# Routed experts: weights loaded once per expert, results gathered back after the last block

## The chip, the cores and the metric

The kernel runs on one core of a Trainium2 chip. The metric is the time of one execution in device microseconds (us); the median of several runs is compared.

## The reference, cut to what matters

A decoder of 12 stages (4 layers of attention, cross attention and feed-forward) adds to a residual of 1024 rows by 256, all float32. Three feed-forward stages are mixtures of experts: layer 0 (here l0f: 16 experts, the 6 best per token), layer 2 (l2f: 8 experts, 2 best, and a shared expert in 4 parts for all tokens) and layer 3 (l3f: 64 experts, 4 best). For l3f:

```python
router_probs = jax.nn.softmax((x @ gate_weight.T).astype(jnp.float32), axis=-1)
top_v, top_i = jax.lax.top_k(router_probs, 4)
top_v = top_v / jnp.clip(top_v.sum(axis=-1, keepdims=True), 1e-12)
combine = jnp.zeros((T, E), dtype=top_v.dtype).at[jnp.arange(T)[:, None], top_i].add(top_v)
gate, up = jnp.split(x @ w1.T, 2, axis=-1)
out += (jax.nn.silu(gate) * up @ w2.T) * combine[:, expert][:, None]
```

## The kernel before, in words

Each stage is a block of code with one program per engine: TensorE (PE), ScalarE (ACT), VectorE (DVE), GpSimd (POOL) and SyncE (SP), which issues most DMAs. Semaphores order them. `experts` (L613) builds the three mixture stages.

**The router.** The normalised tokens h (8 tiles of 128 rows) are stored to the DRAM tensor h_rows by SP. DVE and PE find each token's best experts, count how many blocks of 128 rows each expert needs (blocks sorted by expert), the owner of each block, a slot for each of a token's K choices, and for each block the list of its tokens. The owners are spread over one partition by a matmul against a diagonal and copied to `owners`; SP reads them one by one into a register. The number of groups of four blocks depends on the data; each engine reads it with `group_count` (a value load, L802). Here l0f has 56 blocks (14 groups), l2f 20 (5), l3f 64 (16).

**The blocks.** Each engine walks over the groups with its own `step` four times per group; `by_steps` (L600) writes out the first group, puts the others in a loop (`Fori`, its branch at L606) and the pipeline's end after it. Of a block:
- POOL gathers its 128 rows of h_rows by an indirect DMA (L868), four buffers x;
- PE transposes them (L964, after the wait for x at L962 and for xT), ACT copies them to xT (L1016);
- PE multiplies with the expert's w_in (L973), ACT takes silu of one half (L1022), DVE multiplies it with the other (L1152);
- PE transposes that (L982), DVE copies it (L1146), PE multiplies with w_down (L992), DVE copies y (L1160) and ACT stores it to the stage's DRAM tensor y_rows (L1027).

PE works on four blocks at a time, each a stage further: the transpose of block b stands beside w_in of b-1, the second transpose of b-2 and w_down of b-3.

**The weights.** SP reads the owner of the next block (L821), waits until its place in the ring (16, 16 or 32 places) is free (L827) and until the transfer before on that semaphore has landed (L831), and issues w_in and w_down (L832): one pair per block, whichever expert it is. Before these it stores h and fills that part of y_rows which may stay without a block (L815 to L817: 4, 2 and 16 DMAs of 512 KB), so that every row gathered later is finite.

**The results.** After the last x gather POOL reads, for each choice c, the last block that holds a c-th choice, waits until it is stored (L884 to L887), and issues eight indirect gathers of y_rows (L892), one per tile of tokens, into up to 24 buffers (`BACKS`: 8 own ones, 8 in h and 8 in hT). Only the last choice waits for all blocks. DVE, after its last y, picks the weights of the choices and accumulates each gathered tile into the residual (L1176). The stage ends with the last accumulate.

## Time and profile before

| | |
|---|---|
| median of 3 runs | 1965.07 us (1960.84 to 1971.27) |
| the profiled execution | 1945.26 us |
| its span in the profile | 1943.4 us |
| granted TensorE clock, mean | 0.807 of full speed |
| PE busy | 1126.4 us (58%) |
| DVE busy | 1129.1 us (58%) |
| POOL busy | 591.0 us (30%) |
| DMA | 196.56 MB, mean 101 GB/s |

The profile was taken of a single execution, so its times stand against 1945.26, not against the median. Busy shares are averages over 12 stages with different limits. All times are microseconds from the span's start. A row of a timeline gives start, duration, engine, line, operation, output<-inputs, and in brackets how long the engine was idle before it and what ended the idle time ("issue": nothing that the profile shows). PE's and SP's sequencers (PEldq, SPq) have rows of their own. The expert stages lie at about 264 to 521 (l0f), 1245 to 1412 (l2f) and 1690 to 1932.5 us (l3f).

### The profile page before, as it was taken

The numbers are of one execution on the slowest core, as the hardware profiler recorded it, in microseconds if no ns is written. First come the engines' busy times: TensorE is split into PE (matmuls) and PEld (weight loads), VectorE is DVE, ScalarE is ACT, GpSimd is POOL, SyncE is SP. The second block draws the span as 40 slices with busy tenths as digits, with TensorE's granted clock in tenths as the row PEclk, the third lists the DMA queues.
The fourth block names the chain that finished last, engine by engine and source line by source line (L and its number), as shares of the span: only waits on it lengthen the run. The fifth ranks groups of instructions, "written<-read, shape, count | busy, mean of one in ns | idle before, by whom it ended". The sixth has DMA issues, their size and how long they took to land. (4 is left out here: it accounts for less than half of the span.)

```text
span 1943.4 us, 22726 instructions
## 1 busy us (share of the span) xinstructions
PE 1126.4 (58%) x5644; PEld 710.2 (37%) x5644; DVE 1129.1 (58%) x1878; ACT 473.7 (24%) x881; POOL 591.0 (30%) x616
## 2 busy tenths in 40 slices
PE   5316548994073962551696703698566278648750
PEld 2202125772042730111454502576433034437530
DVE  5759974442462637998875694411457358464324
ACT  2143302220021533320211101332122146403210
POOL 0026613445610103661100072034402022115454
PEclk9669967996586975996898856899878579969985
DMA  6024329983209002421000011244300620088762
GB/s 209 1 90 146 113 77 283 320 285 93 65 9 185 5 27 85 151 87 65 1 0 1 1 13 30 88 134 144 93 5 0 149 49 3 3 279 255 227 192 85
DMA packets 146199, 196.56 MB, mean 101 GB/s; under 512 B 35056, under 2 KB 109954, under 8 KB 145484
## 3 DMA queue, kind: packets, MB, share of 16 engines
q1 hardware_dynamic: 109996, 144.47, 25.3%
q0 software_dynamic: 12608, 31.26, 5.7%
q10 hardware_dynamic: 23520, 19.93, 3.3%
q8 instruction: 35, 0.57, 0.1%
q14 instruction: 40, 0.33, 0.1%
HBM read 153.55 MB, written 41.75 MB: 100 GB/s over the span
## 5 line engine op out<-in xcount | busy, mean ns | idle before, releaser
L163 PE MATMUL psum<-w_ident,h 128*128 128x128 f32 x144 | 32.5, 419 | 156.5 <-DVE h L144 156.5
L1530 DVE TENSOR_REDUCE l3x_neg<-psum 128x2 f32<-128x512 f32 x128 | 80.8, 683 | 59.6 <-PE psum L1402 59.6
L453 PE MATMUL psum<-l0s_conv_out,w_ident 128*128 128x512 f32 x128 | 65.0, 632 | 83.5 <-DVE l0s_conv_out L550 83.5
L453 PE MATMUL psum<-l1s_conv_out,w_ident 128*128 128x512 f32 x128 | 65.4, 636 | 80.0 <-DVE l1s_conv_out L550 80.0
L1505 ACT ACTIVATE l3x_work<-psum 128x512 f32<-128x512 f32 x128 | 72.5, 599 | 75.2 <-PE psum L1424 74.9
L175 ACT ACTIVATE hT<-psum 128x512 f32<-128x512 f32 x40 | 21.7, 595 | 281.2 <-PE psum L163 239.4
L152 POOL TENSOR_SCALAR rstd<-moments 128x8 f32<-128x8 f32 x12 | 2.9, 240 | 281.3 <-DVE moments L140 281.3
L163 PEld LDWEIGHTS psum<-w_ident,h 128*128 128x128 f32 x144 | 29.0, 222 | 160.2 <-DVE h L144 148.0
L419 POOL TENSOR_TENSOR l0s_xpad<-l0s_du,l0s_bc 128x1024 f32<-128x1024 f32 x32 | 75.3, 2354 | 32.5 <-DVE psum L546 32.3
L419 POOL TENSOR_TENSOR l1s_xpad<-l1s_du,l1s_bc 128x1024 f32<-128x1024 f32 x32 | 75.2, 2353 | 32.5 <-DVE psum L546 32.4
L973 PE MATMUL psum<-l0f_w_in,l0f_xT 128*128 (+1 forms) x224 | 78.5, 474 | 11.3 <-issue 11.1
L973 PE MATMUL psum<-l3f_w_in,l3f_xT 128*128 (+1 forms) x256 | 60.1, 360 | 41.1 <-issue 18.0
L868 POOL DMA_INDIRECT l3f_x<-l3f_h_rows,l3f_token_now x64 | 61.5, 961 | 62.7 <-PE psum L964 48.6
L546 DVE TENSOR_TENSOR_SCAN psum<-psum,l0s_xpad 128x1024 f32<-128x1024 f32 x32 | 73.2, 2286 | 5.3 <-POOL l0s_xpad L419 5.3
L546 DVE TENSOR_TENSOR_SCAN psum<-psum,l1s_xpad 128x1024 f32<-128x1024 f32 x32 | 73.2, 2286 | 5.2 <-POOL l1s_xpad L419 5.2
L1146 DVE COPY l0f_gatedT<-psum 88x256 f32<-88x256 f32 x56 | 23.6, 421 | 83.9 <-PE psum L982 49.1
L868 POOL DMA_INDIRECT l0f_x<-l0f_h_rows,l0f_token_now x56 | 53.9, 962 | 60.2 <-PE psum L964 43.4
L1146 DVE COPY l3f_gatedT<-psum 96x128 f32<-96x128 f32 x64 | 18.4, 288 | 91.9 <-PE psum L982 41.2
L453 PEld LDWEIGHTS psum<-l0s_conv_out,w_ident 128*128 128x128 f32 x128 | 22.2, 193 | 126.3 <-DVE l0s_conv_out L550 110.4
L453 PEld LDWEIGHTS psum<-l1s_conv_out,w_ident 128*128 128x128 f32 x128 | 22.4, 195 | 123.3 <-DVE l1s_conv_out L550 107.2
L1402 PE MATMUL psum<-l3x_k_packed,l3x_q_packed 48*128 48x256 bf16 x256 | 43.1, 306 | 34.9 <-DMA l3x_q_packed<-l3x_parts 31.0
L1530 DVE TENSOR_REDUCE l1a_neg<-psum 128x3 f32<-128x384 f32 x64 | 34.6, 556 | 47.1 <-PE psum L1410 46.8
(641 smaller groups left out, 3218.9 us busy)
## 6 DMA issues: line engine op xcount, KB each, us to landing
l0f_w_in<-in_l0f_w_in SPq DMA_DIRECT2D x56, 352.0 KB
l0s_bc<-l0s_scratch SPq DMA_DIRECT2D x16, 1024.0 KB, 5.1
l1s_bc<-l1s_scratch SPq DMA_DIRECT2D x16, 1024.0 KB, 5.2
l3f_w_in<-in_l3f_w_in SPq DMA_DIRECT2D x64, 192.0 KB
l0f_w_down<-in_l0f_w_down SPq DMA_DIRECT2D x56, 176.0 KB
l2f_w_in<-in_l2f_w_in SPq DMA_DIRECT2D x24, 352.0 KB
l3f_y_rows<-h SPq DMA_DIRECT2D x16, 512.0 KB, 6.8
l3f_y_rows<-l3f_y ACTq DMA_DIRECT2D x64, 128.0 KB
```

The lines of the kernel that those rows point to most:

```text
L152: m.pool_order.link(pool, nc.gpsimd.tensor_scalar(m.rstd[:, 0, :], m.moments[:, :, 1], EPS, None, ALU.add))
L163: ins = nc.tensor.transpose(m.psum[:, at:at + P], m.h[:, t, k * P:(k + 1) * P], m.ident[:])
L175: nc.scalar.activation(m.hT[:, k, cols], m.pair(k)[:, cols], ACT.Copy).then_inc(m.hT_ready, 1)
L419: nc.gpsimd.tensor_tensor(drive[c], du[:, c, :], bc[s][:, 0, :], ALU.mult).then_inc(drive_ready, 1)
L453: ins = nc.tensor.matmul(m.pair(2 + c)[:, cols], lhsT=m.ident[:], rhs=rhs[:, cols], start=start, stop=stop, skip_group_check=True)
L546: nc.vector.tensor_tensor_scan(state[c], decay[c], drive[c], 0.0, ALU.mult, ALU.add).then_inc(scanned, 1)
L868: nc.gpsimd.indirect_dma_start(x[s][:], None, h_rows, bass.IndirectOffsetOnAxis(ap=token_now[s // 2][:, s % 2:s % 2 + 1], axis=0)).then_in ...
L973: ins = nc.tensor.matmul(in_ps[d % 2], lhsT=xT[d % 2][:, k, :], rhs=w_in[:, bass.ds(place(base + d), 1), k, :].rearrange("p o x -> p (o x) ...
L1146: nc.vector.tensor_copy(gatedT[d % 2][:], gT_ps[d % 2]).then_inc(gT_ready, 1)
L1402: ins = nc.tensor.matmul(out[:, qt * S:(qt + 1) * S], lhsT=q[:, qt * P:(qt + 1) * P], rhs=k, start=True, stop=True)
L1505: nc.scalar.activation(self.prob[i % 8][:, 0:self.keys], self.bank(3 + i % 3)[:, 0:self.keys], ACT.Exp).then_inc(self.exp_done, 1)
L1530: ins = nc.vector.tensor_reduce(self.neg[k % 2][:, :, hl], bank[:, 0:self.keys].rearrange("p (q k) -> p q k", q=self.maxima), AX_X, ALU.ma ...
```

## The change

- SP loads the weights of every expert once per stage (16, 12 and 64 pairs), at the stage's start and without the owners; at most four experts are in flight, and the semaphore `there` counts the experts that have arrived.
- PE reads the expert of each block itself: two value loads per group of four blocks, each of a word that packs four experts (6 bits each), one for the w_in blocks and one for the w_down blocks, which lag by another two. They stand at the head of the group, ahead of the wait for x, and once more after the loop. Per block PE waits for `there`. The waits for in_loaded and down_loaded go.
- The words are made by one matmul with a constant (`packing`) instead of the diagonal.
- All back gathers wait until all y are stored. Buffers for them: 24, 16 and 16, those in h and hT first.
- y_rows becomes one DRAM tensor for all stages, and all of it (24 DMAs of 512 KB) is filled in stage 0 on SP, after the weight loads, out of ctxT.
- The store of h goes from SP's queue to ACT's, ahead of Exp.
- To make room in SBUF, routing buffers share memory: combine with probs; rest, goes, before, over and slots with hT; picked, x, y and xT with the routing tables; the memset of `before` moves behind the router's matmul. "carry" and "ctxT" leave the group "consts" for a group "spans" that is dropped after stage 10.

```diff
+            m.wait_weights(sp, "spans")
+            for rows in m.y_rows.rearrange("(g b p) d -> g p b d", b=GROUP, p=P):
+                sp.dma_start(rows, m.ctxT[:].rearrange("p (b d) -> p b d", d=D)).then_inc(m.y_filled, 16)
...
+BACKS_OF = {"l0f_": 3 * TILES, "l2f_": 2 * TILES, "l3f_": 2 * TILES}
+EXPERTS_PER_WORD = 64
+EVERY_EXPERT = sum(EXPERTS_PER_WORD ** k for k in range(GROUP))
...
         @block.sync
+            def load(e, k):
+                sp.dma_start(w_in[:, e, :, :]..., source("w_in", e)).then_inc(in_loaded[k], 16)
+                sp.dma_start(w_down[:, e, :, :]..., source("w_down", e)).then_inc(down_loaded[k], 16)
+            def arrived(e):
+                done = e // GROUP * 16 + 16 + EARLIER
+                sp.wait_ge(in_loaded[e % GROUP], done)
+                sp.wait_ge(down_loaded[e % GROUP], done)
+                sp.sem_inc(there, 1)
-            sp.wait_ge(m.h_ready, TILES * (n + 1))
-            sp.dma_start(h_rows.rearrange("(t p) d -> p t d", p=P), m.h[:]).then_inc(h_stored, 16)
-            with sp.Fori(FEWEST, GROUPS) as i:
-                sp.dma_start(y_groups[bass.ds(i, 1)]..., m.h[:, 0:GROUP, :]).then_inc(filled, 16)
-            groups = group_count(sp)
-            def step(base, s, first, last):
-                e = sp.value_load(owners[0:1, bass.ds(base + s, 1)], min_val=0, max_val=E - 1)
...
+            for e in range(E):
+                if e >= GROUP:
+                    arrived(e - GROUP)
+                elif shared:
+                    sp.wait_ge(in_loaded[e], EARLIER)
+                    sp.wait_ge(down_loaded[e], EARLIER)
+                load(e, e % GROUP)
+            for e in range(E - GROUP, E):
+                arrived(e)
...
         @block.gpsimd
+            for s in range(GROUP):
+                pool.wait_ge(y_stored[s], groups * 16 + 16)
+                pool.sem_inc(may_gather, 1)
             for c in range(K):
-                if c < K - 1:
-                    last = pool.value_load(last_block[0:1, c:c + 1], min_val=0, max_val=BLOCKS - 1)
-                for s in range(GROUP):
-                    pool.wait_ge(y_stored[s], ((last + GROUP - s) >> 2 if c < K - 1 else groups) * 16 + 16)
-                    pool.sem_inc(may_gather, 1)
...
         @block.tensor
-                nc.tensor.matmul(owner_row, lhsT=m.w["ones"][:], rhs=owners_diag[:], ...)
+                nc.tensor.matmul(owner_words, lhsT=owner[:], rhs=m.w["packing"][:, :, 0:GROUPS + 1], ...)
+            def experts_of(i):
+                found = []
+                for k in range(2):
+                    word = pe.value_load(words[0:1, k, bass.ds(i, 1)], min_val=0, max_val=(E - 1) * EVERY_EXPERT)
+                    found.append([(word >> 6 * s) & (E - 1) for s in range(GROUP)])
+                return found
...
+                    e = owners[0][s]
+                    pe.wait_ge(there, e + 1)
+                    pe.sem_inc(there_for, 1)
                     pe.wait_ge(xT_ready, base + (d + 1))
-                    pe.wait_ge(in_loaded[d % GROUP], turn(1))
-                        ins = nc.tensor.matmul(..., rhs=w_in[:, bass.ds(place(base + d), 1), k, :]...)
+                        ins = nc.tensor.matmul(..., rhs=w_in[:, bass.ds(e, 1), k, :]...)
...
+                    e = owners[1][s]
-                    pe.wait_ge(down_loaded[d % GROUP], turn(3))
...
-            by_steps(pe, groups, step, 3)
+            owners = experts_of(0)
+            for s in range(GROUP):
+                step(0, s, True, False, owners)
+            with pe.Fori(1, groups) as i:
+                owners = experts_of(i)
+                for s in range(GROUP):
+                    step(i * GROUP, s, False, False, owners)
+            owners = experts_of(groups)
+            for s in range(3):
+                step(groups * GROUP, s, False, True, owners)
...
         @block.scalar
             norm_scalar(m, act, j)
+            act.wait_ge(m.h_ready, TILES * (n + 1))
+            act.dma_start(h_rows.rearrange("(t p) d -> p t d", p=P), m.h[:]).then_inc(h_stored, 16)
             act.wait_ge(less_max, 1)
...
-            act.wait_ge(filled, (GROUPS - FEWEST) * 16)
+            act.wait_ge(m.y_filled, 16 * MOST_GROUPS)
...
         @block.vector
-            nc.vector.tensor_scalar(owners_diag[:], m.ident[:], owner[:, 0:1], None, ALU.mult).then_inc(owner_ready, 1)
-            nc.vector.tensor_copy(owners[:], owner_row[0:1, :]).then_inc(lists_ready, 1)
+            nc.vector.tensor_copy(words[:], owner_words).then_inc(lists_ready, 1)
```

## Rows read from the trace of the kernel before

**Rows 1.** Windows: us, busy us (count) of PE, PEld, DVE, ACT, POOL; clock; DMA; GB/s

```profile
46.00:60.00 14.00, 0.00 (x0) 0.00 (x0) 12.08 (x9) 1.72 (x2) 0.00 (x0) 0.50 0.00 0
...
330.00:430.00 100.00, 100.00 (x484) 74.14 (x483) 43.95 (x122) 28.06 (x81) 42.22 (x61) 1.00 0.99 316
...
1745.00:1800.00 55.00, 49.55 (x271) 39.69 (x269) 24.17 (x87) 19.98 (x61) 32.14 (x47) 0.96 0.85 253
...
1800.00:1870.00 70.00, 48.13 (x251) 37.47 (x251) 24.65 (x86) 18.00 (x57) 30.45 (x43) 0.98 0.76 225
```

**Rows 2.** Timeline, first gathers and transposes: start, duration, instruction [idle <-releaser]

```profile
302.25 1.22 POOL L868 DMA_INDIRECT l0f_x<-l0f_h_rows,l0f_token_now  x1 [0.93 <-POOL l0f_token_now L851]
...
308.34 0.88 PE L964 MATMUL psum<-w_ident,l0f_x 128*128 128x128 f32 x3 [4.88 <-DMA l0f_x<-l0f_h_rows,l0f_token_now]
...
1739.77 1.14 POOL L868 DMA_INDIRECT l3f_x<-l3f_h_rows,l3f_token_now  x1 [0.88 <-POOL l3f_token_now L851]
...
1743.45 0.66 PE L964 MATMUL psum<-w_ident,l3f_x 128*128 128x128 f32 x2 [3.31 <-DMA l3f_x<-l3f_h_rows,l3f_token_now]
```

**Rows 3.** Timeline of l0f's end, 445 to 480 us

```profile
445.07 0.38 PE L964 MATMUL psum<-w_ident,l0f_x 128*128 128x128 f32 x2
...
463.77 2.71 PE L973 MATMUL psum<-l0f_w_in,l0f_xT 128*128 x4 [11.15 <-issue]
...
467.62 0.95 POOL L892 DMA_INDIRECT hT<-l0f_y_rows,l0f_slot_index  x1 [0.30 <-issue]
...
479.80 0.42 DVE L1160 COPY l0f_y<-psum 128x256 f32<-128x256 f32 x1 [1.28 <-PE psum L992]
```

**Rows 4.** SP's instructions of line 832, 1800 to 1872 us

```profile
L832 SPq DMA_DIRECT2D l3f_w_in<-in_l3f_w_in x29: 332/352/353, 1800.0 to 1871.6; - x29
```

**Rows 5.** Timeline of l2f's end, 1381 to 1390 us

```profile
1381.06 0.38 PE L964 MATMUL psum<-w_ident,l2f_x 128*128 128x128 f32 x2
...
1388.37 0.42 DVE L1160 COPY l2f_y<-psum 128x256 f32<-128x256 f32 x1 [0.44 <-PE psum L992]
...
1389.64 1.02 POOL L892 DMA_INDIRECT l2f_back<-l2f_y_rows,l2f_slot_index  x1 [16.23 <-DMA l2f_y_rows<-l2f_y]
```

**Rows 6.** Timeline of l3f's end, 1879 to 1933 us

```profile
1879.62 0.38 PE L964 MATMUL psum<-w_ident,l3f_x 128*128 128x128 f32 x2
...
1903.50 0.42 DVE L1160 COPY l3f_y<-psum 128x256 f32<-128x256 f32 x1 [0.43 <-PE psum L992]
...
1905.95 1.29 POOL L892 DMA_INDIRECT hT<-l3f_y_rows,l3f_slot_index  x1 [13.66 <-DMA l3f_y_rows<-l3f_y]
...
1932.05 0.48 DVE L1176 SCALAR_TENSOR_TENSOR resid<-l3f_back,l3f_weight,resid 128x256 f32<-128x256 f32 x1 [0.76 <-DMA l3f_back<-l3f_y_rows,l3f_slot_index]
```

**Rows 7.** Timeline of l0f's last gather and accumulate

```profile
518.12 0.95 POOL L892 DMA_INDIRECT hT<-l0f_y_rows,l0f_slot_index  x1 [0.30 <-issue]
...
520.89 0.49 DVE L1176 SCALAR_TENSOR_TENSOR resid<-hT,l0f_weight,resid 128x256 f32<-128x256 f32 x1 [0.83 <-DMA hT<-l0f_y_rows,l0f_slot_index]
```

**Rows 8.** DMA issues: queue, count, KB each, median us to landing

```profile
l0f_w_in<-in_l0f_w_in SPq DMA_DIRECT2D x56, 352.0 KB
...
l3f_y_rows<-h SPq DMA_DIRECT2D x16, 512.0 KB, 6.8
```

**Rows 9.** Line 802 on PE's sequencer, whole execution: ns min/median/max, first and last start

```profile
L802 PEldq FUSED_REGOPS  x3: 157/168/171, 300.5 to 1737.2; - x3
...
L802 PEldq TENSOR_LOAD <-l0f_more_turns x1: 488/488/488, 299.9 to 299.9; - x1
```

**Rows 10.** PE's sequencer at a group's head, 355 to 358 us

```profile
L962 PEldq ALU_OP  x1: 36/36/36, 356.3 to 356.3; - x1
...
L973 PEldq FUSED_REGOPS  x2: 46/46/46, 356.7 to 356.9; - x2
```

**Rows 11.** Timeline of PE at the same head

```profile
357.92 0.38 PE L964 MATMUL psum<-w_ident,l0f_x 128*128 128x128 f32 x2
...
358.14 0.46 PE L973 MATMUL psum<-l0f_w_in,l0f_xT 128*128 x1
```

More of the change, by code:

```diff
@@ L610, in by_steps, with experts @@
         step(groups * GROUP, s, False, True)
-def experts(m, n, j, tag, routed, top, rows, chunks, ahead, shared=0, normalize=False, floor=None):
+def experts(m, n, j, tag, routed, top, rows, chunks, shared=0, normalize=False, floor=None):
     nc = m.nc
@@ L674, in experts @@
     up = ring("up", [P, F], 2) if shared else None
-    x = ring("x", [P, D], GROUP)
-    xT = ring("xT", [P, KD, P], 2)
-    w_in = sb(tag + "w_in", [P, ahead, KD, 2 * F])
-    w_down = sb(tag + "w_down", [rows, ahead, chunks, D])
-    place = lambda b: b & (ahead - 1)
-    shared_place = lambda e: ahead - shared + e
+    x, y = ([tables[:, 2 * i * D:2 * (i + 1) * D].bitcast(F32) for i in range(k * GROUP, (k + 1) * GROUP)] for k in range(2))
+    xT = [tables[:, 2 * (2 * GROUP + i) * D:2 * (2 * GROUP + i + 1) * D].bitcast(F32).rearrange("p (k t) -> p k t", t=P)
+          for i in range(2)]
+    w_in = sb(tag + "w_in", [P, routed + shared, KD, 2 * F])
+    w_down = sb(tag + "w_down", [rows, routed + shared, chunks, D])
     silu = ring("silu", [P, F], 2)
@@ L834, in _ @@
-            for g in range(ahead // GROUP):
-                for s in range(GROUP):
-                    step(g * GROUP, s, True, False)
-            with sp.Fori(ahead // GROUP, groups) as i:
-                for s in range(GROUP):
-                    step(i * GROUP, s, False, False)
+            def load(e, k):
+                sp.dma_start(w_in[:, e, :, :].rearrange("p c x -> p (c x)"), source("w_in", e)).then_inc(in_loaded[k], 16)
+                sp.dma_start(w_down[:, e, :, :].rearrange("p c x -> p (c x)"), source("w_down", e)).then_inc(down_loaded[k], 16)
@@ L911, in count @@
                 pe.wait_ge(goes_ready, 1)
-                nc.tensor.matmul(rank, lhsT=m.w["earlier"][:], rhs=goes[:].rearrange("p t e -> p (t e)"),
+                nc.tensor.matmul(rank, lhsT=m.w["earlier"][:], rhs=goes.rearrange("p t e -> p (t e)"),
                                  start=True, stop=False)
@@ L920, in list_owners @@
                 pe.wait_ge(owner_ready, 1)
-                nc.tensor.matmul(owner_row, lhsT=m.w["ones"][:], rhs=owners_diag[:], start=True,
+                nc.tensor.matmul(owner_words, lhsT=owner[:], rhs=m.w["packing"][:, :, 0:GROUPS + 1], start=True,
                                  stop=True).then_inc(owners_filled, 1)
@@ L1058, in _ @@
             dve.wait_ge(routed_ready, 1)
+            o.mark(nc.vector.memset(before[:, 0, :], 0.0))
             o.link(dve, nc.vector.tensor_reduce(row[:], logits[:, :, 0:routed], AX_X, ALU.max))
@@ L2318, in decoder @@
             lambda n, j: state_space(m, 0, n),
-            lambda n, j: experts(m, n, j, "l0f_", routed=16, top=6, rows=88, chunks=2, ahead=16),
+            lambda n, j: experts(m, n, j, "l0f_", routed=16, top=6, rows=88, chunks=2),
             lambda n, j: softmax_attention(m, n, j, "l1a_", heads=16, causal=True),
@@ L2378, in constants @@
     c["ones"] = np.ones((P, P), np.float32)
+    c["packing"] = np.zeros((P, 2, P // GROUP + 1), np.float32)
+    for i, ahead in enumerate((1, 3)):
+        for b in range(P):
+            word, digit = divmod(b + ahead, GROUP)
+            if word <= P // GROUP:
+                c["packing"][b, i, word] = EXPERTS_PER_WORD ** digit
     f = np.arange(P)
```

143 lines of the change are left out of this document (67 added, 76 removed).

## The prediction

> **What bounds the kernel now.** I read the windows first, then the timelines of the three expert stages (l0f, l2f, l3f), then TensorE's sequencer. In l0f's loop TensorE (PE) is busy 100.00 of 100 us [rows 1]: nothing but matmuls sets the pace there, though DMA is also full (share 0.99, 316 GB/s). The first transpose of a block's tokens (L964) starts at 308.34 and the last at 445.07 [rows 2, 3], so 56 blocks take 136.73 / 55 = 2.49 us each. In l3f PE is busy 49.55 of 55 us, then only 48.13 of 70 [rows 1]; at 9 records a block (271 and 251) that is 1.83 us a block, later 2.51. SP issued 29 weight pairs in that later stretch [rows 4], 71.6 / 28 = 2.56 us apart: there SP's value load, four waits and two issues per block are the bound.
>
> The ends of the stages are the second thing to see. In l2f the last transpose starts at 1381.06 and the last copy of y at 1388.37 [rows 5]: 7.3 us, with no gather of results meanwhile. In l0f the same way takes from 445.07 to 479.80, 34.7 us, with PE idle 11.15 us before one matmul, while POOL issues gathers up to 467.62 [rows 3]. In l3f it takes 1879.62 to 1903.50, 23.9 us, also under a burst [rows 6]. So an early gather seems to be paid for by the last blocks. Behind it come the last gathers, 0.95 us each and 0.30 between, 1.25 us apart, and the last accumulate ends 520.89 + 0.49 = 521.4, 3.3 us after the last gather began at 518.12 [rows 7]; in l3f it ends at 1932.5 [rows 6].
>
> **The change part by part.** The profiled execution took 1945.3 us (span 1943.4), 1.0% under the median 1965.07. I sum against 1945.3 and carry the difference to the median.
>
> Weights resident: l0f loads 16 pairs for 56 of 352 KB and its partner [rows 8], and all can be in before the first block. In l0f the gather at 302.25 fed PE at 308.34, 6.1 us later, beside weight loads; in l3f that way took 1739.77 to 1743.45, 3.7 us [rows 2]. In l0f I take the short way, a gain of 2.4 us. In l3f it is the other way round: 64 pairs are now still loading during the first gather, at most 2.4 us worse; I take 1.2. Within l0f's loop the missing loads are worth nothing, since PE is at 100.00 with them; within l3f's second half they are worth the difference between 2.51 and 1.83 us a block, since SP has no work per block left.
>
> Register reads on PE: each group of four blocks now starts with two value loads and up to 8 shifts and masks, ahead of the wait for x. One value load that PE does now shows 0.488 us for the load, then 0.168 [rows 9]. Two are 1.3; with the gaps between them and some of the shifts I take 1.5. What covers it: the sequencer passed L962 at 356.3, and the transpose it sends ran at 357.92 [rows 10, 11], 1.6 us, of which I give 0.2 to sending it: a lead of 1.4. It is done with the next matmul's registers by 356.95, 0.66 behind L962, and the array needs that matmul 0.22 behind the transpose (358.14) [rows 10, 11]. So a boundary costs 1.5 - 1.4 + 0.66 - 0.22 = 0.55 us (rounded up for the new wait and increment ahead of that matmul). Bounds of the insertion: from nothing to 2.5 us (1.5 and two operations for each of eight experts at 0.036 and 0.046, which would be 2.2, and slower loads). Ring masks and two load waits that go are within this. The new wait for the expert finds it long there: l3f's 64 pairs start at the stage's entry, ahead of the whole router, and follow at under the 2.56 us that SP needs now, without its value load. Behind a later matmul ACT (xT, silu) and DVE (gated, y) wait, and behind them only PE again, so the delay isn't multiplied.
>
> Back gathers all at the end: the term with both signs. Of l0f's 48 gathers 24 were hidden, l3f's 16 of 32; l2f's 16 came at the end anyway.
>
> - l0f: first transpose 308.34 - 2.4 = 305.95. Last: + 136.73 + 13 boundaries x 0.55 = 449.8. Tail as l2f's, 7.3 + 0.55 for the reads after the loop: last y copy 457.7. First gather 2.45 behind it, as in l3f (1903.50 to 1905.95) [rows 6]: 460.1. 47 x 1.25 = 58.75, then 3.3: 522.2 against 521.4, **+0.8**. The stall gives 27.4, 24 more exposed gathers take 30, the boundaries 7.7, the first gather of x gives 2.4; and before, the late gathers came slower than an unbroken row (479.80 to 518.12, 38.3 us, for which 2.45 + 23 x 1.25 = 31.2 would do), which I take to be gone as well, 7.1.
> - l2f: 5 boundaries x 0.55, and the first gather 2.45 behind the last copy instead of 1.27 [rows 5]: **+3.9**.
> - l3f: first transpose 1743.45 + 1.2 = 1744.65. 63 x 1.83 + 15 x 0.4 (PE's idle tenth covers some of 0.55) = 121.3: last at 1865.9. Tail 7.3 x 1.83 / 2.49 = 5.4, + 0.5: 1871.8. Gathers from 1874.3, 31 x 1.25 = 38.75, + 3.3: 1916.3 against 1932.5, **-16.2**.
>
> The rest: the fills of the result rows (16 of 512 KB in l3f alone [rows 8]) go to stage 0, where DMA has nothing from 46 to 60 [rows 1]: no cost if they are over before the next stage's traffic; l3f's removed fills make room for the weight loads that move there. All of y_rows' 24 fills at 316 GB/s are an estimate of 40 us, and and SP's 24 issues at 0.35 [rows 4] are 8 us in which its next work (the next stage's loads) waits: 0 to 5 us at that stage's start, I take 0. The h store moves from SP to ACT, whose Exp waits behind it for one issue, not for its landing: 0 to 0.5. One DVE operation and the memset's new place: below 0.5. Sum: 0.8 + 3.9 - 16.2 = **-11.5**, so 1934 for such an execution and 1953 at the median.
>
> **Rivals.**
> 1. Reads hidden. PE's sequencer stood at a wait for DVE before it got its lead; if it runs further ahead, or the reads take 0.9, the 35 boundaries cost nothing: -17 more, 1936. Against it: a lead of 1.4 at 100.00 busy is what the row shows. The Trainium skill, TensorE: Matmul & The Clock Gate, its table at the head, gives TensorE a queue of 64 entries, which would leave room for far more lead; here the trace shows a few matmuls of it, since each block waits for ACT and DVE. By that rule alone the time would be this rival's.
> 2. **Slower:** the reads and their arithmetic hold PE 2.5 us or more at each group's head. Each further microsecond costs 14 + 5 + 16 = 35 us, as all three loops are led by PE once SP is out of the way. At 2.5 instead of 1.5: 1953 + 35 = 1988. It changes the sign from 1.83 us on, and shows beyond the measurement from 2.1. For it: 8 shifts and masks that the compiler may do one by one, and loads of 0.488; against it: they are done once per group, not at each matmul.
> 3. The stall at a stage's end belongs to leaving the loop, not to the gathers. Then l0f keeps 27.4 and l3f 23.9 - 5.9 = 18.0: 1953 + 45 = 1998. Against it l2f leaves the same loop in 7.3 us [rows 5]. For it: l0f's "issue" idle names no releaser. The Trainium skill, Runtime: NRT & Kernel Launch, Instruction fetch mechanics, says that a taken branch to a place outside the fetch window forces a fetch before execution goes on; longer code around the loop would make that likelier. By it the time is this rival's; l2f's exit does not show it.
> 4. It doesn't bring what it says: in l3f POOL or DVE holds the pace at 2.2 us instead of 1.9, 63 x 0.3 = +19: 1972.
>
> **How the numbers follow.** What a measurement of this kernel can tell from no change is about 0.5%, 9.8 us: faster is below 1955, slower above 1975. Forecast (its own range 1942 to 1964, by an insertion of 1.2 to 1.8): 0.45, of it 0.28 faster, 0.17 same. Rival 1: 0.15, faster. Rival 2: 0.2, of it 0.17 slower, 0.03 same. Rival 3: 0.1, slower. Rival 4 and what I didn't think of: 0.1, split 0.03, 0.02, 0.05. Together faster 0.46, same 0.22, slower 0.32. The range goes from below rival 1 to just above rival 2: 1930 to 1990, and leaves out rival 3 and the far end of rival 2.
>
> **What would show it.** Right: last transpose of l0f near 450 and its last y copy 8 us later, no idle of 11 us in between; L964 at group heads late by 0.1 and the next matmul by 0.5; l3f at 1.9 us a block throughout; 48, 16 and 32 gathers in unbroken rows at 1.25. Wrong: PE idle over 1 us at each fourth block (rival 2), none at all (rival 1), idle of many microseconds behind the last transpose with no gathers running (rival 3), gathers slower than 1.25 us in the row, or a later start of stage 1.

## The result and the profile after

The changed kernel took 1975.17 us in the median of 20 runs (1957.48 to 1993.29), the kernel before 1956.59 us in 20 runs (1941.03 to 1974.91). The ratio is 1.0105, 95% interval 1.0071 to 1.0139: **slower by 1%**. The time is inside the range that was given, but the sign is wrong: a gain was the likeliest case. (The forecast of 1953 us was carried to a median of three runs, 1965.07, which the 20 runs put 8.5 us lower; as a ratio it was 0.994.) The profiled execution of the changed kernel has a span of 1958.1 us against 1943.4, 14.7 us more; the granted clock is 0.807 in both.

Where these 14.7 us lie is read from the starts of the stages (first transpose of each stage's normalised tokens, before and after):

| stretch | before | after | difference | forecast |
|---|---|---|---|---|
| l0f | 272.1 | 273.4 | +1.3 | +0.8 |
| l2f | 175.4 | 180.6 | +5.2 | +3.9 |
| l3x (attention, stage ahead of l3f) | 224.5 | 235.3 | +10.8 | none |
| l3f and the end | 246.2 | 246.1 | -0.2 | -16.2 |
| all other stages | | | -2.4 | 0 |

The forecast for these was -11.5 us, so 26.2 us are to be explained: 16.0 in l3f, 10.8 in l3x, 1.8 in l0f and l2f, less the 2.4 of the other stages.

In l0f the forecast holds step by step. The timeline of the changed kernel at l0f's end (start, duration, engine, line, operation, in brackets the idle time before):

```profile
450.29 0.38 PE L972 MATMUL psum<-w_ident,l0f_tables 128*128 128x128 f32 x2
...
458.12 0.42 DVE L1181 COPY l0f_tables<-psum 128x256 f32<-128x256 f32 x1 [0.44 <-PE psum L1002]
...
461.25 0.97 POOL L893 DMA_INDIRECT h<-y_rows,l0f_slot_index  x1 [19.27 <-DMA y_rows<-l0f_tables]
...
520.18 0.94 POOL L893 DMA_INDIRECT l0f_back<-y_rows,l0f_slot_index  x1 [0.30 <-DVE resid L1197]
...
522.88 0.48 DVE L1197 SCALAR_TENSOR_TENSOR resid<-l0f_back,l0f_weight,resid 128x256 f32<-128x256 f32 x1 [0.69 <-DMA l0f_back<-y_rows,l0f_slot_index]
```

The last transpose starts at 450.29 (forecast 449.8), the last y copy at 458.12 (457.7), where [rows 3] had 34.7 us between the two; the first gather at 461.25 (460.1), and 47 gathers later the last one at 520.18, 1.25 us each. The only visible miss is the start of the gathers, 3.13 us behind the last copy instead of 2.45. The same in l2f, where [rows 5] had 1.27:

```profile
1389.66 0.42 DVE L1181 COPY l2f_tables<-psum 128x256 f32<-128x256 f32 x1 [0.44 <-PE psum L1002]
...
1392.77 0.97 POOL L893 DMA_INDIRECT h<-y_rows,l2f_slot_index  x1 [19.26 <-DMA y_rows<-l2f_tables]
```

Together with somewhat dearer heads of groups (the start of each group of four blocks, where the reads stand) that is l2f's 1.3 us of excess.

In l3f nothing was gained. Its windows, with the columns of [rows 1] (us, busy and count of PE, PEld, DVE, ACT, POOL; clock; DMA share; GB/s):

```profile
330.00:430.00 100.00, 98.30 (x456) 69.31 (x454) 41.40 (x114) 26.66 (x76) 39.76 (x57) 1.00 0.33 99
1760.00:1800.00 40.00, 32.65 (x167) 24.89 (x166) 15.33 (x54) 13.63 (x40) 20.90 (x30) 0.94 0.82 254
1800.00:1840.00 40.00, 32.70 (x165) 26.20 (x166) 15.38 (x55) 11.44 (x36) 19.39 (x29) 0.91 0.41 120
1840.00:1870.00 30.00, 24.80 (x125) 20.06 (x123) 12.39 (x43) 8.90 (x28) 14.59 (x20) 0.89 0.43 122
```

165 records in 40 us at 9 a block are 2.18 us a block, where 1.9 was forecast; SP is out of the way (DMA share 0.41 where [rows 1] had 0.76), and PE still is idle for a fifth of the time, at a granted clock of 0.91 and 0.89 instead of 0.98. The end of the stage:

```profile
1893.39 0.38 PE L972 MATMUL psum<-w_ident,l3f_tables 128*128 128x128 f32 x2
...
1901.40 0.42 DVE L1181 COPY l3f_tables<-psum 128x256 f32<-128x256 f32 x1 [0.46 <-PE psum L1002]
...
1904.50 1.26 POOL L893 DMA_INDIRECT h<-y_rows,l3f_slot_index  x1 [16.78 <-DMA y_rows<-l3f_tables]
...
1946.59 0.48 DVE L1197 SCALAR_TENSOR_TENSOR resid<-hT,l3f_weight,resid 128x256 f32<-128x256 f32 x1 [0.76 <-DMA hT<-y_rows,l3f_slot_index]
```

Against its own start l3f's first transpose is where the forecast put it (1759.50, 1.2 us later than before); from there to the last one it took 133.9 us instead of the 121.3 of the sum. PE at one head of a group shows why:

```profile
1848.82 0.38 PE L972 MATMUL psum<-w_ident,l3f_tables 128*128 128x128 f32 x2
...
1849.97 0.60 PE L1002 MATMUL psum<-l3f_w_down,l3f_gatedT 96*128 x2
1852.04 0.43 PE L972 MATMUL psum<-w_ident,l3f_tables 128*128 128x128 f32 x2 [1.47 <-issue]
1852.60 1.11 PE L983 MATMUL psum<-l3f_w_in,l3f_tables 128*128 x4
...
1855.00 1.49 PE L983 MATMUL psum<-l3f_w_in,l3f_tables 128*128 x4
1856.28 0.42 PE L992 MATMUL psum<-w_ident,l3f_gated 128*96 128x128 f32 x1
```

Behind a block that starts at 1848.82 the next one starts at 1852.04, 3.2 us later instead of 1.6, with PE idle for 1.47. And the four matmuls of w_in take 1.11 and 1.49 us (1852.60, 1855.00) where the block before the head had 0.91: the granted clock, 1.00 before the gap, is 0.50 from 1854 to 1856 us (windows with the columns of [rows 1]):

```profile
1846.00:1850.00 4.00, 4.00 (x26) 3.40 (x25) 2.19 (x8) 1.66 (x5) 2.17 (x4) 1.00 0.54 162
1854.00:1856.00 2.00, 2.00 (x8) 1.71 (x8) 0.88 (x3) 0.46 (x2) 0.24 (x2) 0.50 0.37 113
```

What the sequencer does in the gap:

```profile
L962 PEldq FUSED_REGOPS  x3: 46/151/151, 1850.7 to 1851.5; - x3
L962 PEldq TENSOR_LOAD <-l3f_words x2: 298/355/412, 1850.3 to 1851.0; - x2
L962 PEldq SEQ_ASSERT  x2: 18/18/18, 1850.9 to 1851.7; - x2
```

Two loads of 0.30 and 0.41 us and their register work fill 1850.3 to 1851.9. The insertion is 1.6 us, close to the 1.5 of the sum; but nearly all of it is exposed here, as PE's 1.47 us of idle time.

### The profile page after: what moved, and what is told of

It is laid out like the page before. It is cut to its first block and busy times, and to the rows that moved or that the text cites. A ratio compares the mean times of both kernels' runs of the same rounds, so it can differ in the third digit from the quotient of the medians.

```text
span 1958.1 us, 21676 instructions
## 1 busy us (share of the span) xinstructions
PE 1131.6 (58%) x5644; PEld 707.8 (36%) x5645; DVE 1132.6 (58%) x1875; ACT 474.3 (24%) x881; POOL 583.4 (30%) x616
## 5 line engine op out<-in xcount | busy, mean ns | idle before, releaser
L425 POOL TENSOR_TENSOR l1s_xpad<-l1s_du,l1s_bc 128x1024 f32<-128x1024 f32 x32 | 75.3, 2355 | 32.5 <-DVE psum L552 32.3
L425 POOL TENSOR_TENSOR l0s_xpad<-l0s_du,l0s_bc 128x1024 f32<-128x1024 f32 x32 | 75.3, 2354 | 32.5 <-DVE psum L552 32.3
L872 POOL DMA_INDIRECT l3f_tables<-l3f_h_rows,l3f_token_now x64 | 61.7, 964 | 62.1 <-PE psum L972 37.0
L983 PE MATMUL psum<-l0f_w_in,l0f_tables 128*128 x224 | 78.3, 472 | 2.1 <-issue 0.9
L872 POOL DMA_INDIRECT l0f_tables<-l0f_h_rows,l0f_token_now x56 | 54.1, 965 | 80.9 <-PE psum L972 75.9
L459 PEld LDWEIGHTS psum<-l0s_conv_out,w_ident 128*128 128x128 f32 x128 | 22.2, 193 | 126.2 <-DVE l0s_conv_out L556 110.4
L459 PEld LDWEIGHTS psum<-l1s_conv_out,w_ident 128*128 128x128 f32 x128 | 22.5, 196 | 124.4 <-DVE l1s_conv_out L556 108.2
L983 PE MATMUL psum<-l3f_w_in,l3f_tables 128*128 x256 | 62.1, 369 | 4.2 <-issue 2.9
L1551 DVE TENSOR_REDUCE l1a_neg<-psum 128x3 f32<-128x384 f32 x64 | 34.7, 556 | 46.3 <-PE psum L1431 45.7
```

The source lines that it names most:

```text
L425: nc.gpsimd.tensor_tensor(drive[c], du[:, c, :], bc[s][:, 0, :], ALU.mult).then_inc(drive_ready, 1)
L459: ins = nc.tensor.matmul(m.pair(2 + c)[:, cols], lhsT=m.ident[:], rhs=rhs[:, cols], start=start, stop=stop, skip_group_check=True)
L872: nc.gpsimd.indirect_dma_start(x[s], None, h_rows, bass.IndirectOffsetOnAxis(ap=token_now[s // 2][:, s % 2:s % 2 + 1], axis=0)).then_inc(x ...
L983: ins = nc.tensor.matmul(in_ps[d % 2], lhsT=xT[d % 2][:, k, :], rhs=w_in[:, bass.ds(e, 1), k, :].rearrange("p o x -> p (o x)"), start=(k = ...
L1551: ins = nc.vector.tensor_reduce(self.neg[k % 2][:, :, hl], bank[:, 0:self.keys].rearrange("p (q k) -> p q k", q=self.maxima), AX_X, ALU.ma ...
```

## The experiments

All ratios are to the kernel before, run beside each of them on the same chip, with 95% intervals. The kernel before itself had two levels: a median of 1952, 1956 and 1956 us in the second, fifth and sixth set, as in the result above, but 1906, 1909 and 1912 in the first, third and fourth. The level does not belong to a chip: by the record sets 1 and 2 ran on the same one. So a ratio is compared within its set, and parts of the kernel by their own duration, each from one profile. The ratios are estimates from all runs of a set and differ from the quotient of the two medians by up to 0.3%. "l3x" is the length of that stage as in the table above.

**Set 1: the two kernels again, the reads, the early gathers.**

Kernel before, unchanged:

> The kernel before, unchanged, for the spread of its profile. Theory P (the 10.8 us that stage l3x is longer after the change belong to the changed kernel): l3x's norm-to-norm time again near 224.5 us, l1a's likewise near 523.7. Rival C (chance of an execution): l3x varies by several us between two profiles of the same kernel, up to 10. Ratio 1.000 within 0.005.

Measured: 1903.64 us, ratio 0.9999 (0.9967 to 1.0032); l3x 228.7, l1a (the attention stage behind l0f) 523.7 as before. It is 40 us under its first profile, 15 us of them in l0f and 28 in l3f. Timeline of this run at l0f's end:

```profile
442.36 0.97 POOL L892 DMA_INDIRECT l0f_back<-l0f_y_rows,l0f_slot_index  x1 [1.42 <-DMA l0f_y_rows<-l0f_y]
...
448.59 0.38 PE L964 MATMUL psum<-w_ident,l0f_x 128*128 128x128 f32 x2
...
455.81 0.42 DVE L1160 COPY l0f_y<-psum 128x256 f32<-128x256 f32 x1 [0.44 <-PE psum L992]
```

The gathers start at 442.36, among the last blocks, and yet the last y copy comes 7.2 us behind the last transpose, not 34.7 as in [rows 3]. l3f's tail (last transpose to last y copy) is 6.4 us instead of 23.9. The stalls from which the sum took a gain of 45 us are not there in this run. Nor is SP the bound of l3f here: its first to last transpose take 119.0 us instead of 136.2. SP's issues of l3f's weights from the fourteenth to the thirty-third pair, in the first profile of the kernel before and in this one:

```profile
L832 SPq DMA_DIRECT2D l3f_w_in<-in_l3f_w_in x20: 4/345/719, 1751.2 to 1800.0; - x20
```

```profile
L832 SPq DMA_DIRECT2D l3f_w_in<-in_l3f_w_in x20: 345/345/356, 1738.0 to 1773.1; - x20
```

That is 2.57 us a pair against 1.85. So SP is 3 us ahead of PE at the thirty-third pair in the one and 22 us in the other, and though both need 2.5 us a pair from there on, only in the first does PE have to wait for it. What slows SP in the first is not shown.

Changed kernel, unchanged:

> The changed kernel, unchanged. Theory P: l3x again near 235 us. Rival C: anywhere between 224 and 236. Both: last transpose of l0f at 450, l3f from its norm to the end again 235 us; ratio to the kernel before 1.007 to 1.014.

Measured: 1982.0 us, ratio 1.0417 (1.0359 to 1.0475), outside the expected 1.007 to 1.014; l3x 238.8 us. The changed kernel itself is within 7 us of its first median; it is the kernel before that is 50 us faster here. l0f's last transpose starts at 449.94; l3f took 249.5 us.

Without the reads:

```diff
             def experts_of(i):
-                found = []
-                for k in range(2):
-                    word = pe.value_load(words[0:1, k, bass.ds(i, 1)], ...)
-                    found.append([(word >> 6 * s) & (E - 1) for s in range(GROUP)])
-                return found
+                return [[(i * GROUP + (s - lag)) & (E - 1) for s in range(GROUP)] for lag in (1, 3)]
```

> Changed kernel in which PE takes the expert from the block's number (as the ring's place before) instead of the two value loads and the unpacking; some blocks use another expert's weights. Theory R (TensorE's sequencer is what sets the pace at the groups' heads, and in l3f everywhere, so that each head costs the full insertion): l3f's 15 heads give 1.6 us each, 24 us, l0f's 13 heads 0.45 each, 6 us, l2f 2: together about 32 us under the changed kernel, ratio to the kernel before 0.994. Rival G (the heads cost little, l3f's pace is set by POOL's gathers at 2.0 us a block): under 10 us, ratio above 1.003.

Measured: 1938.46 us, ratio 1.017 (1.011 to 1.023): 43 us less than the changed kernel of the set, more than the 32 of theory R. From the first to the last transpose l3f takes 109.6 us instead of 138.1, l0f 135.4 instead of 144.8. With the same gathers on POOL a block of l3f takes 109.6 / 63 = 1.74 us, so rival G falls. The altered values also sent more tokens' blocks to l2f (24 instead of 20), which costs this kernel some 6 us.

Early gathers in the changed kernel:

```diff
-            for s in range(GROUP):
-                pool.wait_ge(y_stored[s], groups * 16 + 16)
-                pool.sem_inc(may_gather, 1)
             for c in range(K):
+                if c < K - 1:
+                    last = pool.value_load(last_block[0:1, c:c + 1], min_val=0, max_val=BLOCKS - 1)
+                for s in range(GROUP):
+                    pool.wait_ge(y_stored[s], ((last + GROUP - s) >> 2 if c < K - 1 else groups) * 16 + 16)
+                    pool.sem_inc(may_gather, 1)
```

> Changed kernel with the gathers of results again as soon as a choice's last block is stored (PE's reads and resident weights stay). Theory B (gathers beside the last blocks stall PE): the stalls come back in l0f (last transpose to last y copy 30 us or more instead of 7.7) and in l3f (over 20 instead of 7.9), while 24 and 16 gathers are hidden (30 and 20 us): the time within 5 us of the changed kernel. Rival W (the stalls belonged to the weight loads or SP's waits beside the gathers): no stalls, and 30 + 20 less some 5 us are gained: ratio to the kernel before near 0.987.

Measured: 1952.35 us, ratio 1.0251 (1.0172 to 1.033), 30 us less than the changed kernel of the set. No stall: l0f's last y copy comes 8.0 us behind the last transpose. Where the stalls are absent, gathering late costs 30 us. Rival W's ratio (0.987) is missed because it reckoned with a kernel before that stalls: in this set it doesn't either. l3x is long too, 242.1 us.

**Set 2: where the tiles lie, late gathers alone, a hybrid.** The new constant `packing` is 264 bytes a partition. With it all tiles behind it, l3x's among them, start at a multiple of 32 bytes and of nothing larger; before, l3x_q_packed lay at 110080, a multiple of 512, now at 110368.

Kernel before, shifted:

```diff
         for name, shape in WEIGHTS[group]:
             m.weight(group, name, shape)
+        if group == "routing":
+            m.sb("shift", [P, 72])
```

> Kernel before, with one unused SBUF tile of 288 bytes a partition behind the routing constants, so that l3x's and l3f's tiles lie where the changed kernel has them (l3x_q_packed at 110368 instead of 110080 bytes, a multiple of 32 alone instead of 512). Theory A (where the packed tiles lie in SBUF sets how fast their DMAs are written): l3x takes 235 to 240 us from norm to norm instead of 224 to 229, its packing DMAs 0.95 to 1.05 us each by the median instead of 0.69, and the ratio is 1.004 to 1.007. Rival D (the DRAM scratch's place, or the traffic ahead of it, does it): l3x 224 to 229 us, ratio 1.000.

Changed kernel, set right (the same two lines with 56 instead of 72):

> Changed kernel with 224 unused bytes behind the routing constants, so that the later tiles lie at multiples of 512 bytes again. Theory A: l3x back to 224 to 229 us from 235 to 242, 10 us less in all, ratio to the changed kernel 0.995. Rival D: l3x stays at 235 to 242.

Measured: 1964.79 us, ratio 1.0051 (1.0011 to 1.0091) for the shifted kernel before; 1952.95 us, ratio 1.0016 (0.9966 to 1.0065) for the changed kernel with its tiles set right. l3x takes 242.0 and 222.2 us. SP's DMAs into that tile (count, min/median/max ns to issue one), in the kernel before, the changed one, the shifted and the aligned one, each in a fence:

```profile
L1322 SPq DMA_DIRECT2D l3x_q_packed<-l3x_parts x36: 396/687/2174, 1516.8 to 1559.2; - x36
```

```profile
L1343 SPq DMA_DIRECT2D l3x_q_packed<-l3x_parts x36: 442/958/2119, 1521.3 to 1578.4; - x36
```

```profile
L1322 SPq DMA_DIRECT2D l3x_q_packed<-l3x_parts x36: 372/1011/2718, 1527.1 to 1583.5; - x36
```

```profile
L1343 SPq DMA_DIRECT2D l3x_q_packed<-l3x_parts x36: 360/574/1795, 1530.0 to 1568.4; - x36
```

And PE's longest wait of the stage in the changed and in the aligned kernel (total us, times, longest):

```profile
PE psum L1423 <- DMA l3x_q_packed<-l3x_parts: 37.8, 1, 37.8
```

```profile
PE psum L1423 <- DMA l3x_q_packed<-l3x_parts: 29.4, 1, 29.4
```

Shown in both directions for the stage: an unused tile makes the kernel before slower there, and another brings the changed kernel back to the level of the kernel before. Rival C has a share too: over all profiles with a multiple of 512 l3x is 215.3 to 228.7 us long. l1a does the same packing at a multiple of 64 before and of 32 after, and shows nothing (median 431 ns each time); set 5 comes back to that.

Kernel before with late gathers alone (the edit of `early_back` the other way round):

> Kernel before with all gathers of results after the last stored block, nothing else. Where the kernel before has no stalls in its last blocks (as in its second profile): l0f 13 us longer and l3f 16 us, ratio 1.013 to 1.017. Where it has them (as in its first profile, tails of 34.7 and 23.9 us) and the early gathers make them: tails of 7 and 6 us and a ratio near 0.998; if they have another cause, the tails stay at 34.7 and 23.9 and the ratio is 1.02 or more.

Measured: 1955.16 us, ratio 1.0006 (0.9959 to 1.0052). This is a set with stalls: the shifted kernel before, whose gathers are early, has PE idle 12.56 us in l0f's tail and its last y copy 34.7 us behind the last transpose. With late gathers:

```profile
450.42 0.38 PE L961 MATMUL psum<-w_ident,l0f_x 128*128 128x128 f32 x2
...
457.65 0.42 DVE L1157 COPY l0f_y<-psum 128x256 f32<-128x256 f32 x1 [0.44 <-PE psum L989]
...
460.79 0.97 POOL L889 DMA_INDIRECT l0f_back<-l0f_y_rows,l0f_slot_index  x1 [18.01 <-DMA l0f_y_rows<-l0f_y]
```

```profile
446.15 0.39 PE L964 MATMUL psum<-w_ident,l0f_x 128*128 128x128 f32 x2
...
467.64 2.71 PE L973 MATMUL psum<-l0f_w_in,l0f_xT 128*128 x4 [12.56 <-issue]
...
480.86 0.42 DVE L1160 COPY l0f_y<-psum 128x256 f32<-128x256 f32 x1 [1.28 <-PE psum L992]
```

7.2 us against 34.7. So in this set early gathers do stall the last blocks, late ones remove it, and the exposed gathers eat the gain, as the sum had it (-27.4 against +30).

Hybrid: kernel before, with resident weights in l0f and l2f, one word of six experts (4 bits each) per group, early gathers, `packing` 512 bytes wide:

```diff
+                word = pe.value_load(owners[0:1, bass.ds(i, 1)], ...)
+                return [(word >> 4 * k) & (E - 1) if k else word & (E - 1) for k in range(GROUP + 2)]
...
-                    pe.wait_ge(in_loaded[d % GROUP], turn(1))
+                    e = found[s + 2]
+                    pe.wait_ge(there, e + 1)
```

> Kernel before with resident weights in l0f and l2f alone, PE reading one word per group (six experts of 4 bits) instead of two, h stored by ACT, early gathers, fills and l3f as before, packing constant of 512 bytes a partition so that nothing loses its place. One value load is 0.75 us of insertion against a lead of 1.4: Theory R: heads of groups in l0f no later than before, l0f 4 to 8 us shorter (first x lands 2 to 4 us sooner), l2f within 2 us, ratio 0.996. Rival: the extra register work for each block (0.3 us) also counts, 56 x 0.1 to 0.2 us given back, ratio 1.000 or above.

Measured: 1951.9 us, ratio 0.9996 (0.9957 to 1.0034). l0f is 3.4 us shorter than in the first profile of the kernel before, l2f equal, l0f's tail stalls (33.2 us). 4 to 8 us had been expected in l0f; in the whole no difference can be told.

**Set 3: pricing the reads on aligned tiles.**

> Changed kernel with its later tiles at multiples of 512 bytes, once more, as the base for the two that follow on this chip. Ratio to the kernel before 1.00 where the kernel before has stalls in its last blocks, 1.03 where it has none.

Measured: 1960.72 us, ratio 1.0256 (1.0213 to 1.0298).

Without the reads (the edit of `no_reads`):

> The same with the experts taken from the block's number instead of the two value loads per group (some blocks use another expert's weights). Theory R (PE's sequencer sets l3f's pace, each read counts in full there): last transpose in l3f 24 to 28 us sooner after the first, l0f 9 us, together 35 to 43 us less than the base, ratio to it 0.979 to 0.982. Rival (much of the gain seen before came with that run's chip): under 20 us less.

Measured: 1924.57 us, ratio 1.0091 (1.005 to 1.0133), 36 us under its base although l2f again has 24 blocks. From the first to the last transpose l3f takes 110.4 us instead of 140.7.

One read instead of two:

```diff
+                earlier_word = None if isinstance(i, int) and i == 0 else pe.snap(kept, min_val=0, max_val=MOST)
+                word = pe.value_load(words[0:1, 0, bass.ds(i, 1)], min_val=0, max_val=MOST)
+                digit = lambda w, s: (w >> 6 * s) & (E - 1)
+                down = [digit(earlier_word, s + 2) ... for s in range(2)] + [digit(word, s) for s in range(2)]
...
                 for s in range(GROUP):
                     step(i * GROUP, s, False, False, owners)
+                pe.reg_mov(kept, word)
```

> The base with one value load per group instead of two: the w_down experts of the group's first two blocks come from the word of the group before, kept in a register. Theory R: half the insertion goes, 0.75 us at 15 heads of l3f = 11 us, in l0f the rest fits under the lead of 1.4 us: 13 x 0.6 = 8 us, l2f 2: 18 to 22 us less than the base, ratio to it 0.990. Rival (the sequencer's many small register operations per block count, not the loads): under 8 us less.

Measured: 1916.42 us, ratio 1.0062 (1.0022 to 1.0101), 44 us less than the base, twice what was expected. Some 13 of them are l3x's spread (215.5 against 228.5); l3f is 28.3 us shorter, where 11 had been expected, l0f 5.3, l2f 3.2. The windows of l3f with two reads, and with one:

```profile
1800.00:1840.00 40.00, 32.07 (x156) 25.63 (x155) 14.81 (x51) 10.77 (x34) 18.39 (x28) 0.87 0.40 116
```

```profile
1790.00:1830.00 40.00, 36.78 (x205) 29.07 (x205) 19.58 (x68) 14.38 (x45) 24.21 (x35) 1.00 0.54 149
```

and PE at a head with one read:

```profile
1802.55 0.39 PE L976 MATMUL psum<-w_ident,l3f_tables 128*128 128x128 f32 x2
...
1804.56 0.43 PE L976 MATMUL psum<-w_ident,l3f_tables 128*128 128x128 f32 x2 [0.42 <-issue]
1805.12 0.91 PE L987 MATMUL psum<-l3f_w_in,l3f_tables 128*128 x4
```

The gap is 0.42 us instead of 1.47, and the clock stays at 1.00 where it was 0.87. The matmuls behind the head take 0.91 us, not 1.1 to 1.5. From the first to the last transpose l3f takes 140.7 us with two reads, 114.9 with one and 110.4 with none. Over the 15 heads the second read costs 25.8 / 15 = 1.7 us each, for 0.75 us of sequencer time, and the first only 4.5 / 15 = 0.3 us: more than half of the first is covered, nothing of the second. At 36 records a group the two windows give 9.2 and 7.0 us a group; 0.9 of these 2.2 us is longer busy time (0.206 against 0.179 us per record), which goes with the lower clock, the rest is idle time.

One read, early gathers:

> one_read with the gathers of results again as soon as a choice's last block is stored. Where gathers beside the last blocks stall them: within 6 us of one_read; where they don't: 25 to 30 us less than one_read, at or a little under the kernel before.

Measured: 1893.34 us, ratio 0.9925 (0.9886 to 0.9964): faster than the kernel before, and than the changed one in each of its runs. 23 us less than with late gathers; l0f's stage takes 248.4 us, the shortest so far.

**Set 4: the last two once more**, in a set at the lower level again.

> One read per group, early gathers, aligned tiles, once more and perhaps on another chip. Where the kernel before stalls in its last blocks (its time near 1950): the early gathers stall this kernel too (l0f's last transpose to last y copy above 25 us, l3f's above 18), ratio about 0.985, since l3f's pace no longer hangs on SP. Where it does not (near 1907): 0.990 to 0.995 again.

> The same with late gathers. Where the kernel before stalls: no stalls here, l0f as in the changed kernel less 5 us, l3f 40 us less than the changed kernel's, together ratio 0.975 to 0.985, level with the early version or under it. Where it does not: 1.003 to 1.010 again.

Measured: ratios 0.9913 (0.9855 to 0.997) and 1.0028 (0.9965 to 1.0091), as in set 3.

**Set 5: which multiple counts.** The kernel before with 64 unused bytes, behind the routing constants in the first, behind l1a's constants in the second.

> Kernel before with an unused tile of 64 bytes behind the routing constants: l3x_q_packed at 110144 (a multiple of 64, no longer of 256), and, by the same shift, l1a_q_packed at 151552 (a multiple of 4096; before 151488, of 64 alone). Theory T (what counts is a start at a multiple of 256, where each run of 512 bytes takes two transactions instead of three): l3x 235 to 242 us as with 32, its packing DMAs 0.95 us or more by the median; l1a's first wait for its packing (22.5 us) and its stage stretch (523.6 us) get shorter, by 2 to 8 us. Rival S (only a start off 64 is slow): l3x 215 to 229, l1a as before.

> Kernel before with the same 64 bytes behind l1a's constants: l1a_q_packed at 151552, a multiple of 4096, l3x where it was (110080, of 512). Theory T: l1a's stretch 2 to 8 us shorter than 523.6, l3x 215 to 229 us, ratio 0.996 to 0.999. Rival N (l1a's packing is not bound by how it is written: median 431 ns at 64 as at 32): l1a's wait within 1 us of 22.5, ratio 1.000.

Measured: 1963.9 us, ratio 1.0012 (0.9965 to 1.006), and 1946.42 us, ratio 0.9943 (0.9901 to 0.9985). l3x is 239.9 us at the multiple of 64 and 225.1 at 512: 64 is as bad as 32, rival S falls. l1a's stretch, now at 4096 in both, is 521.8 and 516.3 us where the kernel before has 523.7. Its first wait for the packing, in the kernel before (the profile of set 1) and in `l1a_256`:

```profile
PE psum L1408 <- DMA l1a_q_packed<-l1a_parts: 23.1, 1, 23.1
```

```profile
PE psum L1408 <- DMA l1a_q_packed<-l1a_parts: 20.3, 1, 20.3
```

2.8 us shorter, with the issues at 431 ns as ever. `shift_64` has 21.9, the first profile of the kernel before 22.5. Over all profiles this wait is 20.3 to 21.9 us in the three whose tile lies at a multiple of 256 (set 6 has the third) and 22.4 to 24.6 in the other 17; the stretch of l1a is 516.3 to 521.8 and 520.7 to 531.8, which overlap. So l1a's tile had not lain at the good place in the kernel before, which fits that the shift by 288 bytes showed nothing there. The Trainium skill (DMA: Bandwidth & Descriptors, How a descriptor splits into AXI transactions) says that a transaction, also one that reads less than 256 bytes, has to start at a multiple of 256, so that for a descriptor which doesn't start there the first one begins at the multiple below. By that account, which speaks of reads, a run of 512 bytes is three transactions instead of two, as an estimate. These times agree with 256 as the multiple that counts, but no run has a tile at a multiple of 128 alone, and the transactions themselves are in no row here.

**Set 6: everything together.** One read, early gathers, packing cut to its one word (132 bytes) and padded so that both packed tiles start at a multiple of 256 and of nothing larger; beside it one read with late gathers.

> one_read_early with the packing constant cut to the one word that is read and both attentions' packed tiles at multiples of 256 and of nothing larger. Theory T (256 is what counts): l3x 215 to 229 us at a multiple of 256 as at 512, l1a's stretch 516 to 522 instead of 524 to 528, ratio 0.985 to 0.990 where the kernel before has no stalls; where it has them the early gathers stall this one too: 0.975 to 0.985. If 512 is needed: l3x 235 or more, ratio near 0.995.

> One read, late gathers, tiles at 512. Where the kernel before stalls (near 1952): no stalls here, l3f near 223 us instead of 246 to 248: ratio 0.978 to 0.985. Where it does not (near 1908): 1.003 to 1.010 again.

Measured: 1927.31 us, ratio **0.9829 (0.9748 to 0.9909)**, and 1917.99 us, ratio **0.9812 (0.9731 to 0.9894)**. Both are faster than the kernel before beside them, which no version with two reads was in any set (the changed kernel had 1.0105 beside a kernel before of this level, 1.0016 with its tiles set right). l3x is 229.6 us at a multiple of 256 (the upper end of the good group, 6 us under the bad one). This is a set with stalls, and only the first has early gathers. PE in its l0f tail:

```profile
441.28 0.38 PE L978 MATMUL psum<-w_ident,l0f_tables 128*128 128x128 f32 x2
...
450.64 0.66 PE L998 MATMUL psum<-w_ident,l0f_gated 128*88 128x128 f32 x2 [6.57 <-DVE l0f_gated L1181]
...
467.34 2.71 PE L989 MATMUL psum<-l0f_w_in,l0f_tables 128*128 x4 [14.33 <-issue]
```

14.33 us idle before one matmul, and 32.5 us from the last transpose to the last y copy; in l3f 23.0. `one_read_3` has 7.3 and 5.5, and takes 1918 us as it did in the sets without stalls (1916 and 1918). Its l3f is 224.9 us long, against 246 to 249 for each version with two reads or with SP's ring of weights in l3f, in sets of this kind.

Over all 20 profiles l3x took 215.3 to 229.6 us in the 14 with a multiple of 256 or more, and 235.3 to 242.1 in the 6 without.

## Why the prediction was wrong

- **The step that failed** is the one for l3f: "63 x 1.83 + 15 x 0.4 (PE's idle tenth covers some of 0.55)". The idle tenth of [rows 1] was read as slack that covers a longer sequence of instructions. It is the reverse: in l3f the matmuls of a block are short (1.48 us from one block to the next in the trace after), and the sequencer is what PE waits for: it reaches the wait at a block's head three times within 1845.0 to 1848.2 us, 1.6 us a block, in this row of its instructions (first and last start):

```profile
L970 PEldq EVENT_SEMAPHORE  x3: 51/51/51, 1845.0 to 1848.2; - x3
```

So it has little lead, and the lead of 1.4 us that [rows 10, 11] show for l0f was carried to a stage where it isn't. Without reads a head in l3f is no longer than another block (1.7 and 1.8 us from transpose to transpose); with one read it is 2.0 to 2.1, with two 3.1, and there the clock goes too (0.84 to 0.94 in the windows of `after` and `aligned_again`, instead of 1.00 in those of `one_read`). Measured price of both reads in l3f: 28.5 us (138.1 against 109.6 from the first to the last transpose, 1.9 a head), where the sum had 15 x 0.4 = 6. The loads themselves were sized right (1.5 against 1.6). Rival 2 named the right place, but put its condition in the wrong number: not reads of 2.5 us, but no cover for reads of 1.6. Rival 4's 2.2 us a block came true (2.13 here, 2.19 in set 1), but not by its cause: with the same work on POOL and DVE and no reads a block takes 1.74.
- **The step that was missing** is l3x: 264 bytes of a constant moved every later tile. Without it (`after_aligned`) the change is at 1.0016 in a set with stalls. "One DVE operation and the memset's new place: below 0.5" was the only line on what the change moves in memory. Of the 1.05% between 0.5 and 0.9 is this: 0.5 is what the same shift costs the kernel before (`before_shift`), and 10.8 of 1943.4 us are 0.55%; 0.9 is 1.0105 against 1.0016, from two sets of runs and with intervals that nearly touch.
- **l0f was right** in each of its steps within 1.2 us, the tail of 7.3 + 0.55 among them, and the price of a head: 0.55 forecast, (144.8 - 135.4) / 13 = 0.72 measured. Rival 1 is refuted: two reads are not hidden (one is: l0f's transposes take 136.1 to 137.3 us with one). That the stage came out near zero is in part luck, as the next point shows.
- **The gathers at the end**: right in that the early ones stalled the last blocks of the profile shown (`before_late` against `before_shift`), and right that it is a trade of about zero there. What the single profile could not show: in three sets of six there are no stalls, and then late gathers cost 30 us (`early_back`) and 23 (`one_read_early` against `one_read`). A kernel with late gathers is the same in both kinds of set (1975 and 1982 with two reads, 1918 and 1916 with one); it is the early ones that move by 34 to 50. Rival 3, a stall that belongs to leaving the loop, is refuted by the tails of 7.2 and 7.3 us in `before_late` and `one_read_3`, and by where the stall begins. In the first profile of the kernel before, PE's matmuls of w_in for the last block but one are recorded behind the last transposes of [rows 3]; ACT waits for the results of both, and runs its loop's branch (L606) only after that:

```profile
445.29 1.35 PE L973 MATMUL psum<-l0f_w_in,l0f_xT 128*128 x4
...
462.86 0.38 ACT L1016 ACTIVATE l0f_xT<-psum 128x256 f32<-128x256 f32 x1 [15.14 <-remote]
472.65 0.32 ACT L1022 ACTIVATE l0f_silu<-psum 128x176 f32<-128x176 f32 x1 [9.41 <-remote]
```

```profile
L606 ACTq COMPARE_BRANCH  x1: 40/40/40, 473.2 to 473.2; - x1
```

So ACT gets PE's results 17 and 26 us after PE's records of them, in the midst of its loop ("remote" is a semaphore whose source the profile doesn't name). The end of a matmul's record is modelled, so PE's 11.15 us of "issue" in [rows 3] need not be time in which PE had nothing to do. The rule of the Trainium skill that stood beside rival 3 (Runtime: NRT & Kernel Launch, Instruction fetch mechanics) has no row here that bears it out.
- **l2f** 3.9 against 5.2, a term mis-sized: the first gather comes 3.1 us behind the last copy, not 2.45 (3.1 to 3.4 in every stage with late gathers).
- The fills in stage 0 and h's store on ACT cost nothing visible: stages 0 and 1 together 256.5 and 257.3 us.

Left open: what makes the early gathers hold up PE's results in one set of runs and not in another, with the same program; no experiment was made on it. It is also open what slows SP's ring loads in l3f in these sets (2.57 against 1.85 us a pair); the stage is 28 us longer by it and by the tail, of which the tail is 17.4.

## What to carry to other kernels

An idle share of a tensor engine is slack only as far as its sequencer runs ahead; look at how long the sequencer needs for one round of waits and register work, and compare it with the matmuls of that round, before adding a register read to the loop. A second read cost 1.7 us per group for 0.75 us of instructions, since nothing covered it and the gap also took the clock, where the first had cost 0.3; keeping one word in a register gave the loop back. And when a constant of odd size is added, look where the tiles behind it come to lie: round it up so that they keep a multiple of 256 bytes. Trust a stall that one profile shows only when a second one has it too.

## What the runs showed that was not expected

- DMAs from a DRAM scratch into an SBUF tile (36 a stage, 24 of them of 64 KB: 16 partitions x 8 runs of 512 bytes) took SP 0.93 to 1.07 us each (median) where the tile began at a multiple of 32 or 64 bytes alone, and 0.54 to 0.74 at one of 256 or 512; the stage was 6 to 27 us longer, from the nearest to the farthest pair of profiles. 64 unused bytes made the kernel before faster by 0.6% (`l1a_256`), of which the wait in l1a explains 2.8 us.
- With PE idle for 1.5 us at a group's head (two reads) the granted clock was 0.84 to 0.94 over windows of l3f's loop (`after`, `aligned_again`), 0.50 right behind such a gap; with 0.4 us (`one_read`) it was 1.00.
- The same program ran at 1906 and at 1952 us in two sets on the same chip; in the profiles of the two levels the difference lies in l0f's last blocks (27 us, of which 15 are left at the stage's end) and in l3f (28 us).
